# Context products of an attention layer in four sets per group instead of six, with a fourth buffer of exponentials

## What is computed

```python
xn = _layernorm(x)
q  = xn @ Wq                        # 32 heads x 16
k, v = split(xn @ Wkv)              # 8 groups x 16, shared by 4 query heads
s  = softmax(causal(q k^T) / 4) v   @ Wo + bo
h  = silu(lora(xn, gate_w)) * lora(xn, up_w)      # 1376 hidden features
g  = silu(lora(h, down_w))
out = x + s * g
```

## Time and profile before

| | |
|---|---|
| median of 3 runs | 1152.95 us (1144.7 to 1156.6) |
| the profiled execution | 1163.04 us, of which 1161.2 us are the span of the trace |
| PE, DVE, ACT, POOL busy | 91%, 54%, 40%, 10% |
| granted clock of PE, mean | 0.923 of full speed |

### The profile page before, as it was taken

The page is one execution under the profiler, slowest core; times in us unless marked ns, Lnnn a source line. Parts: engine busy times, 40 slices in busy tenths (PEclk is TensorE's granted clock), DMA queues, the critical chain, the costliest instruction groups (busy, mean ns, idle before and its releaser), DMA issues.

```text
span 1161.2 us, 16175 instructions
## 1 busy us (share of the span) xinstructions
PE 1056.7 (91%) x5668; PEld 607.1 (52%) x5668; DVE 631.7 (54%) x1752; ACT 464.8 (40%) x917; POOL 115.3 (10%) x159
## 2 busy tenths in 40 slices
PE   4749997999999999999999999999878878799897
PEld 3535453555555555555555555554344434456685
DVE  6636453565655565655665565565545545432344
ACT  3312343544544444444444453444433324353121
POOL 3000000010000101010100000010000101112011
PEclk9979796999999999999999998997678879899899
DMA  6435344131321313130312223124031242133552
GB/s 190 136 108 192 124 148 133 42 91 39 92 75 55 84 36 92 38 87 30 91 54 76 70 60 86 39 75 137 29 95 46 61 115 72 47 102 97 157 166 97
DMA packets 118862, 103.49 MB, mean 89 GB/s; under 512 B 41352, under 2 KB 86408, under 8 KB 118784
## 3 DMA queue, kind: packets, MB, share of 16 engines
q1 hardware_dynamic: 118784, 102.47, 29.5%
HBM read 60.20 MB, written 41.42 MB: 88 GB/s over the span
## 4 chain that ended last, share of the span: by engine, by line
PE 79%; DVE 7%; DMA 5%; ACT 4%; SPq 3%; issue 2%; POOL 0%; POOLq 0%; DVEq 0%; ACTq 0%
PE bank L197 17%; PE o L904 12%; PE bank L198 12%; PE bank L199 12%; PE st L887 11%; PE s L868 8%; DMA q<-scratch_q 2%; PE bank L759 2%; ACT prob L1092 2%; DMA hid_in<-scratch_hid 2%; PE bank L788 1%; PE bank L725 1%; PE bank L755 1%; DVE junk L1318 1%; PE bank L784 1%
## 5 line engine op out<-in xcount | busy, mean ns | idle before, releaser
L1092 ACT ACTIVATE prob<-st 128x512 f32<-128x512 f32 (+1 forms) x640 | 328.1, 551 | 454.6 <-PE st L887 454.2
L1318 DVE CUSTOM_DVE_ANT_0 junk<-s,mask 128x128 bf16<-128x128 f32 (+3 forms) x512 | 230.3, 488 | 208.1 <-PE s L868 207.2
L1321 DVE TENSOR_REDUCE part_max<-s 128x1 f32<-128x512 f32 x256 | 164.8, 686 | 138.6 <-PE s L868 138.4
L868 PE MATMUL s<-k,q 64*128 64x512 f32 (+3 forms) x768 | 153.2, 394 | 42.7 <-DMA q<-scratch_q 25.6
L887 PE MATMUL st<-q,k 64*128 64x512 f32 (+3 forms) x768 | 158.4, 436 | 17.6 <-ACT prob L1092 16.0
L427 POOL TENSOR_SCALAR_AFFINE_SELECT prob<-prob 128x512 f32<-128x512 f32 x128 | 79.8, 635 | 891.3 <-ACT prob L1092 891.3
L197 PE MATMUL bank<-x_hi,w_hi 128*128 128x512 f32 (+1 forms) x352 | 162.7, 462 | 0.0
L904 PE MATMUL o<-prob,v 128*32 128x512 f32 (+3 forms) x1536 | 158.8, 535 | 0.0
L887 PEld LDWEIGHTS st<-q,k 64*128 64x128 f32 x768 | 69.4, 191 | 139.1 <-issue 90.0
L199 PE MATMUL bank<-x_hi,w_lo 128*128 128x512 f32 (+1 forms) x352 | 138.9, 395 | 0.0
L198 PE MATMUL bank<-x_lo,w_hi 128*128 128x512 f32 (+1 forms) x352 | 138.6, 394 | 0.0
(11 more groups left out here) (103 smaller groups left out, 962.1 us busy)
## 6 DMA issues: line engine op xcount, KB each, us to landing
q<-scratch_q SPq DMA_DIRECT2D x64, 200.0 KB
scratch_hid<-hid SPq DMA_DIRECT2D x40, 256.0 KB, 2.1
hid_in<-scratch_hid SPq DMA_DIRECT2D x16, 640.0 KB, 4.3
scratch_q<-proj_hi SPq DMA_DIRECT2D x32, 256.0 KB
scratch_o<-o_sb SPq DMA_DIRECT2D x32, 256.0 KB, 2.1
k<-scratch_k SPq DMA_DIRECT2D x32, 192.0 KB
scratch_q<-proj_lo SPq DMA_DIRECT2D x16, 256.0 KB
ctx<-scratch_o SPq DMA_DIRECT2D x64, 64.0 KB
```

Of the source, the lines that this page charges most:

```text
L868: pe.matmul(sb_[(p + odd) % S_BANKS][:, 0:wd], q[half, g % 2, h // 2, qt * P:(qt + 1) * P], k[half, g % 2, k0:k0 + wd], start=True, stop=T ...
L1092: nc.scalar.activation(prob[:, job % 3, h, 0:JOB_COLS[j]], st[at % ST_BANKS][:, 0:JOB_COLS[j]], ACT.Exp, scale=float(HD) ** -0.5).then_inc ...
L1318: ins = dve.tensor_tensor_reduce(junk[:, n % S_BANKS, 0:wd], bank_[:, 0:wd], mask[:, C - wd:C], 1.0, LOWEST, ALU.add, ALU.max, part[:, h, ...
L1321: ins = dve.tensor_reduce(part[:, h, qt, dst:dst + 1], bank_[:, 0:wd], AX.X, ALU.max)
```

## The change

`prob` gets a fourth buffer (`PROBS = 4`), and the waits that go with it move by one job. The context products of a group are done in four sets: jobs 0, 1, 2 in slot 14; 3, 4 in slot 22; 5, 6 in slot 30; 7, 8, 9 in slot 2 of the next round. Before there were six: 0 in slot 6, 1 and 2 in slot 14, 3 and 4, 5 and 6, 7 and 8 in slot 38, 9 in slot 2 of the next round. `neg_pad` shrinks from 128 to 32 columns for each of its two buffers, so the stationary operand of `turn_max` is 128x32 in place of 128x128, and it writes 32 partitions of the score bank.

```diff
-TOGETHER = {0: [0], 2: [1, 2], 4: [3, 4], 6: [5, 6], 8: [7, 8], 9: [9]}
+TOGETHER = {2: [0, 1, 2], 4: [3, 4], 6: [5, 6], 9: [7, 8, 9]}
+PROBS = 4
...
-        prob = sbuf(ctx, "prob", [P, 3, REP, C])
+        prob = sbuf(ctx, "prob", [P, PROBS, REP, C])
...
-        neg_pad = sbuf(ctx, "neg_pad", [P, 2, P])
-        neg_parts = neg_pad[:, :, 0:REP * QT].rearrange("p a (h j t) -> p a h j t", h=REP, j=2)
+        neg_pad = sbuf(ctx, "neg_pad", [P, 2, REP * QT])
+        neg_parts = neg_pad[:, :, :].rearrange("p a (h j t) -> p a h j t", h=REP, j=2)
...
-                pe.transpose(sb_[p % S_BANKS][:, 0:P], neg_pad[:, n % 2], ident[:, :]).then_inc(m_turned, 1)
+                pe.transpose(sb_[p % S_BANKS][0:REP * QT, 0:P], neg_pad[:, n % 2], ident[:, :]).then_inc(m_turned, 1)
...
-                if h == 0 and job >= 3:
-                    act.wait_ge(pv_done, job - 2)
-                nc.scalar.activation(prob[:, job % 3, h, 0:JOB_COLS[j]], st[at % ST_BANKS][:, 0:JOB_COLS[j]], ACT.Exp,
+                if h == 0 and job >= PROBS:
+                    act.wait_ge(pv_done, job - PROBS + 1)
+                nc.scalar.activation(prob[:, job % PROBS, h, 0:JOB_COLS[j]], st[at % ST_BANKS][:, 0:JOB_COLS[j]], ACT.Exp,
```

More of the change, by code:

```diff
@@ L425, in attention @@
                         for col in DIAGONAL[j]:
-                            blk = prob[:, job % 3, :, col:col + P]
+                            blk = prob[:, job % PROBS, :, col:col + P]
                             ins = pool.affine_select(out=blk, in_=blk, compare_op=ALU.is_ge, fill=0.0, base=0,
@@ L905, in context @@
                                        v[:, i % 3, kt].rearrange("p a e -> p (a e)"),
-                                       prob[:, job % 3, h, col:col + q1 - q0],
+                                       prob[:, job % PROBS, h, col:col + q1 - q0],
                                        start=kt == 0, stop=j in HALF_END)
```

## The result

The kernel after takes 1145.66 us (median of 20 runs, 1137.89 to 1155.91) against 1156.61 us (median of 20 runs, 1140.41 to 1163.92) for the kernel before. The ratio is 0.9941, with a 95% interval of 0.9914 to 0.9969: 0.6% faster, some 7 us, where I had forecast 4 us slower. This ratio and those of the experiments leave out the runs of each kernel that lie over 1.5% above its fastest one, which takes more runs from before than from after; the medians of all runs give 0.9905, and I read the gain as 7 to 11 us.

A forecast was written before the change was run, and what follows sets the result against it. PE's own sequence was taken as the bound from 210 to 780 us. Terms -4.5 + 2.9 + 1.5 + 5 = +4.9 us on the median 1152.95 us gave 1158, rounded down to 1157 us; range 1144 to 1170.

The forecast's parts named there:

- The sets: PE's sequence: 32 context sets fewer at 0.14 us each beside their columns, -4.5 us at full clock.
- The turn: Slots 16 and 6: narrow turn before a background product takes 0.26 us, giving +2.9 us and 0.
- The rival with the free turn: Turn at 0.08 us: -7.4 + 1.5 = -6 us, 1147 us with the clock unchanged; chance 0.13.
- lost cover: Slots 38 and 6 lose 1.86 and 1.00 us of products, so PE waits for exponentials: +1.5 us.
- The fourth buffer: Buffer reuse in slots 16 and 4: PE waits for no copy, costed at nothing.
- The clock: Folds from 210 to 780 us: six more run unbroken, 3 more falls at 1.7 us, +5 us.

The follow-up runs named there:

- e6: Kernel before with ten sets per group, one per job, three buffers and the wide turn; ratio to before 0.9929 [0.9886, 0.9972].
- e7: Kernel after with the six sets of before, so four buffers and the narrow turn alone; ratio to before 1.0004 [0.9944, 1.0064].
- e1: Kernel before with the narrow turn alone (neg_pad of 32 columns), six sets and three buffers; ratio to before 1.0005 [0.9967, 1.0043].
- e2: Kernel after with a wide turn (120 stationary columns), four sets and four buffers; ratio to before 0.9965 [0.9926, 1.0004].

## Why the prediction was wrong

**The sets: right in size by the rows.** The set of three took 2.29 us, as 0.14 us per set had it, and 32 sets are 4.5 us. As times the sets don't fit so closely: the long stage fell by 8 to 9 us, of which the rows of sets and turns give 6, and it grew by only 4 to 5 us in e6, where 44 more sets at 0.14 us are 6.

**The turn: wrong in sign.** The step that failed is "with 32 stationary columns it has the form of a context product ... I expect the 0.26 us there". I took the 0.26 us of the earlier trace rows for a change of form and carried it over to the reverse pair. A narrow turn costs 0.04 us before a background product, so slot 16 gives 16 x 0.044 = 0.7 us in place of costing 2.9, and slot 6 gives 16 x (0.26 - 0.04) = 3.5 in place of 0. So by the rows the term of +2.9 us is -4.2, and with the sets -8.7; the rest fell by 10.2. The measured 0.04 us lies outside my bounds of 0.08 to 0.26. The rival with the free turn came nearest, at 1147 us, with some luck: its turn at 0.08 us was too dear, its lost cover came to nothing, and its unchanged clock came of two shifts that cancel. The trace of before held a hint. A wide turn took 0.26 us before a fold product too, whose operand has 128 columns like the turn's own:

```profile
206.71 0.33 PE L875 MATMUL s<-ident,neg_pad 128*128 128x128 f32 x1
206.97 0.48 PE L759 MATMUL bank<-bT,a_low 16*128 16x128 f32 x2
```

The price belonged to the follower.

**The fourth buffer: right. The lost cover: too dear.** e7 and e1 have the same rest, with and without the buffer. PE's waits from 210 to 780 us went from 3.0 us to 3.8, where I had said 4.5, but not for the reason that I gave. e1, which has all six sets in their places and the narrow turn alone, has the 3.8 us too, and e2, which has four sets and the wide turn, has 2.9; first e1, then e2:

```profile
PE st L887 <- ACT prob L1092: 3.8, 13, 0.8
```

```profile
PE st L888 <- ACT prob L1093: 2.9, 8, 0.7
```

So in this stage the products taken out of slots 38 and 6 cost no wait, and the term of +1.5 us measured 0.

**The clock: the cause right where I looked, the size too small, and incomplete over the run.** Folds with no set in their middle lose the clock more often, 16 of 30 against 6 of 54, near the two in four that I had. I had forecast five falls from 210 to 780 us in place of two. Both traces of after have three, but of 6.8, 10.2 and 6.8 us, where I had reckoned with 3.4. The low time in the long stage rose by 24 us (10 to 34), a cost of 12 us where I had put 5. From 210 to 780 us alone it is 8 us; the rest is a fall at 202 us, and the third trace of before has one there too. But the same change set a large set among the down folds, where the low clock fell from 39, 18 and 35 us to 8, a gain of about 11 us. That stage isn't in my account of the clock at all. Over whole runs the clock costs 77.5 us against 74.5 to 78.7: the term of +5 us measured about +1, within its error. So the forecast of +4.9 us became -9 in the means over all runs: of the 14 us between them 7.1 are the turn, about 4 the clock and 1.5 the lost cover; some 1 us, less than the errors, stays unassigned.

## What to carry to other kernels

When PE never idles, two currencies count: the time at full clock and what the low clock costs. Split every run into them before comparing; here ten sets had some 4 us more work than six in the long stage and ran 8 to 10 us faster. But the split is a rough one: check it on a stage where PE doesn't wait. Try spreading the dense products through stretches of transposes and of products with few rows, before saving on the number of switches between them. Trace a kernel more than once before calling a place safe from a fall of the clock. And don't carry the price of a pair of instructions over to the reversed pair: measure the pair, and leave the bounds open on the cheap side, for here the step was half of the cheapest that the trace had shown.

## What was not expected of the hardware

- A narrower stationary operand shortens the step to the next product by 0.46 ns per column, with no step at the change of form between 32, 64, 120 and 128 columns.
- PE busy in every microsecond doesn't hold the clock. From 498.9 to 509.1 us of the kernel after, with transposes, products of 16 rows and scores of 64 rows before it, it was at the 1.2 GHz level, in both traces of this kernel in the same place.
- More switches can be faster: ten sets in place of six, 0.9929 of the time.
- A dense set in the middle of a fold makes a fall of the clock rarer and doesn't exclude it: 6 of 54 such folds had one.
